# Reading the gates' destination scores from PSUM, and scatter sums that share one bank, in a graph layer

## The reference

```python
h = jnp.maximum(_layernorm(x, axis=-1), 0.0)
xs, xd = h[src], h[dst]
att = jax.nn.sigmoid(xs @ W_att[:d] + xd @ W_att[d:] + b_att)
messages = (xs @ W_msg + b_msg) * att
aggregated = jax.ops.segment_sum(messages, dst, num_segments=num_nodes)
gi = aggregated @ W_ih.T + b_ih
gh = h @ W_hh.T + b_hh
# r, z, n as in a GRU cell; h_new = (1 - z) * n + z * h
return x + gamma * (h_new - mean) * rsqrt(var + eps) + beta
```

## Time and profile before

| | us |
|---|---|
| median of 3 runs | 2257.26 |
| lowest and highest | 2253.13, 2259.02 |
| span of the profiled execution | 2256.1 |
| TensorE's granted clock in it, mean | 0.965 of full |

### The profile page before, as it was taken

One profiled execution on the slowest core, in us unless ns is written; L12 is line 12 of the kernel. 1 busy time (PEld: TensorE's weight loads), 2 busy tenths in 40 slices (PEclk: granted clock), 3 DMA queues, 4 the chain that ended last, 5 costly groups with the idle time before them and its releaser, 6 DMA issues.

```text
span 2256.1 us, 53903 instructions
## 1 busy us (share of the span) xinstructions
PE 2055.7 (91%) x18202; PEld 1994.3 (88%) x18202; DVE 2012.9 (89%) x4413; ACT 1996.3 (88%) x6980; POOL 1660.4 (74%) x1578
## 2 busy tenths in 40 slices
PE   3536999999999999999999999999999999999997
PEld 3525999999999999999999999999999999999996
DVE  5967899999999999999999999999999999999974
ACT  1368999999999999999999999999999999999943
POOL 4575777777777777777777777777777777777760
PEclk8865999999999999999999999999999999999998
DMA  6862222222222222222222222222222222222236
GB/s 164 237 172 62 56 60 62 59 60 60 62 62 62 63 58 64 61 63 59 63 59 62 59 61 60 63 60 62 60 61 63 59 62 60 61 61 64 58 108 231
DMA packets 167473, 171.57 MB, mean 76 GB/s; under 512 B 79462, under 2 KB 131736, under 8 KB 166944
## 3 DMA queue, kind: packets, MB, share of 16 engines
q0 software_dynamic: 49856, 102.96, 20.3%
q1 hardware_dynamic: 114564, 61.63, 10.5%
q10 hardware_dynamic: 2776, 3.52, 0.7%
HBM read 141.32 MB, written 26.65 MB: 74 GB/s over the span
## 4 chain that ended last, share of the span: by engine, by line
ACT 53%; PE 23%; DVE 14%; issue 7%; DMA 2%; SPq 1%; POOL 0%; ACTq 0%; DVEq 0%
ACT big L901 41%; PE ps L1456 12%; ACT gate_ring L897 9%; DVE big L1200 4%; PE ps L1441 4%; PE ps L1451 3%; DVE gate_ring L1184 2%; DVE key_hot L1170 1%; PE ps L1462 1%; PE ps L1463 1%; DVE lo_hot L1163 1%; DMA big<-in_x_dram 1%; DVE big L1129 1%; DMA row_ring<-node_table,set_idx 1%; ACT n_blk L906 1%
## 5 line engine op out<-in xcount | busy, mean ns | idle before, releaser
L773 POOL DMA_INDIRECT row_ring<-node_table,set_idx x1480 | 1571.8, 1062 | 473.4 <-issue 334.5
L901 ACT ACTIVATE big<-set_score,big 128x128 f32<-128x128 f32 x5096 | 1633.2, 394 | 81.0 <-PE ps L1456 80.7
L1456 PE MATMUL ps<-big 128*128 128x128 f32 x10192 | 1447.4, 281 | 0.0
L1456 PEld LDWEIGHTS ps<-big 128*128 128x128 f32 x10192 | 1265.0, 193 | 0.0
L1200 DVE TENSOR_TENSOR big<-ps,big 128x784 f32<-128x784 f32 x832 | 802.0, 964 | 10.2 <-ACT big L901 5.4
L1441 PE MATMUL ps<-gate_ring,row_ring 128*128 128x64 f32 x2960 | 534.8, 263 | 78.0 <-DVE gate_ring L1184 72.7
L1441 PEld LDWEIGHTS ps<-gate_ring,row_ring 128*128 128x128 f32 x2960 | 454.0, 194 | 124.4 <-DVE gate_ring L1184 110.7
L1184 DVE SCALAR_TENSOR_TENSOR gate_ring<-lane,set_rel,gate_ring 128x64 f32<-128x64 f32 x1480 | 412.9, 279 | 140.1 <-ACT gate_ring L897 135.0
L897 ACT ACTIVATE gate_ring<-set_win,row_ring 128x64 f32<-128x64 f32 x1480 | 493.2, 341 | 30.5 <-DMA row_ring<-node_table,set_idx 27.3
L1451 PE MATMUL ps<-key_hot,lo_hot 128*128 128x196 bf16 x3328 | 425.8, 250 | 14.4 <-DVE key_hot L1170 9.5
L1170 DVE TENSOR_TENSOR key_hot<-lane_key,set_key 128x1568 bf16<-128x1568 bf16 x416 | 402.0, 966 | 0.0
(11 more groups left out here) (129 smaller groups left out, 917.2 us busy)
## 6 DMA issues: line engine op xcount, KB each, us to landing
row_ring<-node_table,set_idx POOLq DMA_INDIRECT x1480
big<-in_x_dram SPq DMA_DIRECT2D x48, 256.0 KB, 5.6
h_blk<-hT_spill SPq DMA_DIRECT2D x97, 64.0 KB
node_table<-big SPq DMA_DIRECT2D x24, 258.0 KB
hT_spill<-big SPq DMA_DIRECT2D x24, 256.0 KB, 4.8
out_dram<-big SPq DMA_DIRECT2D x24, 256.0 KB
set_win<-dst_scores SPq DMA_DIRECT2D x148, 32.0 KB
set_score<-dst_scores SPq DMA_DIRECT2D x52, 64.0 KB
```

The source lines that it names most:

```text
L773: nc.gpsimd.indirect_dma_start(row_ring[:, t % ROWS_RING, :], None, table, bass.IndirectOffsetOnAxis(ap=set_idx[:, t // SET % 2, t % SET:t ...
L901: return nc.scalar.activation(a_buf[b % 2][:, h, :], set_score[:, b % 2, :], ACT.Sigmoid, bias=m_all[:, h, D:ROW])
L1456: return nc.tensor.matmul(ps[:, AM_BANK, 0:P], m_all[:, h, 0:D], a_buf[b % 2][:, h, :], start=h == 0, stop=h == HI - 1)
```

## The change

ACT copies what the gates read into PSUM. `keep_score(b)` copies the 128 destination scores of block `b` into bank 6 (two places, `ps_score`), once a block; `keep_window(g)` copies the 64 scores of group `g`'s window into the same bank (four places, `ps_dst_scores`), once a group, in the step of the group before's fifth tile. `gate` and `dense_gate` read these in place of `set_win` and `set_score`. SP's next `load_score` waits for the copy, not for the block's gates.

Bank 6 is thereby taken from the scatter sums. All groups now sum in bank 5, in four places of 64 columns (`ps_window`). `GROUP_LAG` goes from 3 to 1: DVE adds a group in the step of the next group's first tile, right after that tile's mask, when the group's last tile may just have been scattered. PE doesn't scatter the next group's first tile in its own step but one tile later, ahead of the second tile (`scattered_at`), and waits there until the group before has been added; before, it waited for the group before that one.

```diff
-GROUP_LAG = 3
+GROUP_LAG = 1
+def scattered_at(t):
+    if t < GROUP or t % GROUP > 1:
+        return (t,)
+    return (t - 1, t) if t % GROUP else ()
...
+        def ps_window(g):
+            return ps[:, SP_BANK, (g % GROUPS_S) * WIN:(g % GROUPS_S + 1) * WIN]
+        def ps_score(b):
+            return ps[:, SCORE_BANK, (b % 2) * P:(b % 2 + 1) * P]
+        def ps_dst_scores(g):
+            return ps[:, SCORE_BANK, 2 * P + (g % GROUPS_S) * WIN:2 * P + (g % GROUPS_S + 1) * WIN]
...
-                    sp.wait_ge(gates_dense, u + 1)
+                    sp.wait_ge(scores_kept, u + 1)
                     load_score(u + 2)
...
+            def keep_score(b):
+                act.wait_ge(score_loaded[b % 2], 16 * (b // 2 + 1))
+                nc.scalar.copy(ps_score(b), set_score[:, b % 2, :]).then_inc(scores_kept, 1)
+            def keep_window(g):
+                if g % GROUPS_S == 0:
+                    set_ready(act, g // GROUPS_S)
+                nc.scalar.copy(ps_dst_scores(g), set_win[:, g // GROUPS_S % 2, g % GROUPS_S, :]).then_inc(windows_kept, 1)
             def gate(t):
-                if t % SET == 0:
-                    set_ready(act, t // SET)
+                if t % GROUP == 0:
+                    act.wait_ge(windows_kept, t // GROUP + 1)
...
-                nc.scalar.activation(gate_ring[:, t % GATES_RING, :], set_win[:, t // SET % 2, t % SET // GROUP, :], ACT.Sigmoid,
+                nc.scalar.activation(gate_ring[:, t % GATES_RING, :], ps_dst_scores(t // GROUP), ACT.Sigmoid,
+                if t % GROUP == 4 and t // GROUP + 1 < GROUPS:
+                    keep_window(t // GROUP + 1)
             def dense_gate(b, h):
-                return nc.scalar.activation(a_buf[b % 2][:, h, :], set_score[:, b % 2, :], ACT.Sigmoid, bias=m_all[:, h, D:ROW])
+                return nc.scalar.activation(a_buf[b % 2][:, h, :], ps_score(b), ACT.Sigmoid, bias=m_all[:, h, D:ROW])
...
             def add_group(g, base):
-                nc.vector.tensor_tensor(window, ps[:, SP_BANK + g % 2, 0:WIN], window, ALU.add).then_inc(groups_added, 1)
+                nc.vector.tensor_tensor(window, ps_window(g), window, ALU.add).then_inc(groups_added, 1)
...
-                        if t % GROUP == GROUP_LAG and t > GROUP:
+                        if t % GROUP == 0 and t:
                             add_group(t // GROUP - 1, bases[t // GROUP - 1])
...
                 if t % GROUP == 0:
-                    wait_reuse(pe, groups_added, g - 1)
+                    wait_reuse(pe, groups_added, g)
...
-                        scatter(t)
+                    for of in scattered_at(t) if t is not None else ():
+                        scatter(of)
```

More of the change, by code:

```diff
@@ L70, in groups_before @@
 def groups_before(u, s):
-    return GROUPS if u == BLOCKS and s > LAST_TILES + GROUP_LAG else max(0, tiles_before(u, s) - GROUP_LAG - 1) // GROUP
+    return GROUPS if u == BLOCKS and s > LAST_TILES + GROUP_LAG else max(0, tiles_before(u, s) - GROUP_LAG) // GROUP
+def scattered_at(t):
+    if t < GROUP or t % GROUP > 1:
+        return (t,)
+    return (t - 1, t) if t % GROUP else ()
 def groups_needed(j):
@@ L315, in gnn_program @@
         ps = ctx.enter_context(nc.psum_tensor("ps", [P, 8, 512], F32))
-        AM_BANK, SP_BANK, GRU_BANK = 4, 5, 7
+        AM_BANK, SP_BANK, SCORE_BANK, GRU_BANK = 4, 5, 6, 7
         def ps_rows(b, j):
@@ L386, in gnn_program @@
         score_loaded = sems("score_loaded", 2)
+        scores_kept = sem("scores_kept")
+        windows_kept = sem("windows_kept")
         gathered = sems("gathered", ROWS_RING)
@@ L913, in _ @@
             keep_edges(11)
-            act.wait_ge(score_loaded[0], 16)
+            keep_score(0)
+            act.wait_ge(scores_kept, 1)
             act.wait_ge(sparse_stored, 32)
             for h in range(HI):
+                if h == HI - 6 * GATES_EARLY:
+                    keep_window(0)
                 if h == HI // 2:
@@ L937, in _ @@
                     b, i = dense_at(u, s)
+                    if u == 0 and s == 4:
+                        keep_score(1)
+                    if 0 < b < BLOCKS - 1 and i == 20:
+                        keep_score(b + 1)
                     if 0 < b < BLOCKS and i < PARTS:
                         if i == 0:
-                            act.wait_ge(score_loaded[b % 2], 16 * (b // 2 + 1))
+                            act.wait_ge(scores_kept, b + 1)
                         if b > 1:
@@ L1187, in add_group @@
             def add_group(g, base):
[L1189 removed]
+                dve.wait_ge(tiles_summed, (g + 1) * GROUP)
                 wait_reuse(dve, groups_added, g)
                 window = agg[:, bass.ds(base, WIN)]
[L1192 removed]
+                nc.vector.tensor_tensor(window, ps_window(g), window, ALU.add).then_inc(groups_added, 1)
             def keep_pairs(b, q):
@@ L1439, in scatter @@
                 if t % GROUP == 0:
-                    wait_reuse(pe, groups_added, g - 1)
-                nc.tensor.matmul(ps[:, SP_BANK + g % 2, 0:WIN], row_ring[:, t % ROWS_RING, 0:D],
+                    wait_reuse(pe, groups_added, g)
+                nc.tensor.matmul(ps_window(g), row_ring[:, t % ROWS_RING, 0:D],
                                  gate_ring[:, t % GATES_RING, :], start=t % GROUP == 0, stop=t % GROUP == GROUP - 1
@@ L1482, in _ @@
                     t = tile_at(u, s)
-                    if t is not None:
-                        scatter(t)
+                    for of in scattered_at(t) if t is not None else ():
+                        scatter(of)
                     if u < BLOCKS and s % PER_BEAT in (0, 2):
```

1 line of the change is left out of this document (removed).

## The result

| | us |
|---|---|
| before, median of 4 runs | 2257.89 |
| after, median of 4 runs (lowest, highest) | 2275.70 (2270.50, 2281.81) |
| ratio, 95% interval | 1.0087 [1.0072, 1.0103] |
| span of the profiled execution after | 2268.8 |

What follows compares the result with a forecast made beforehand. POOL's gathers, 38.6 us a block, and ACT's loop with PE at about that pace were taken as bounds. From a span of 2256.1 us, -12 at the start and -8 in pace gave 2236, so 2237 us; range 2198 to 2268.

Steps and rivals of the forecast that it cites:

- What bounds the kernel before: Block loop: POOL gathers without a stop, 38.6 us a block, and ACT's loop with PE closes at about that pace.
- the loss: What a batch's gathers lose beside DVE's one-hots: 0.43 us before, forecast to fall by 0.02 us a batch.
- ACT's reads: Gates reading PSUM save 0.042 us each, 5.3 us a block; the added copies cost 1.0 us a block.
- ACT's busy time: Sign expected in the profile: ACT some 12 points less busy, with dense gates 0.25 us apart.
- Start, -12 us: Up to 360 us: faster gates cut POOL's waits for scatters, 12 us saved, bounds -4 and -22.
- The end: After the last gather: the late landing of the last rows keeps its length, 0 us.
- Pace, -8 us: Block loop: one batch in ten more has a wait between lo and key one-hots, 0.35 becoming 0.16 us; 8 us saved.
- POOL gets slower: Rival, block loop: waits between one-hots vanish, gathers lose 0.50 us a batch, 2274 us; chance 0.15.
- The moved adding, 0 on the path: Group ends: 51 of 146 make DVE wait, 32 us in all, taken up by DVE's slack; 0 on the path.
- the slot that is freed later: Group's first tile: its row's slot is freed about 1 us later in one tile of ten; 0 us.
- PE takes over: Rival, block loop: gathers lose 0.33 us a batch, PE sets the pace, 2207 us, 2188 at bare pace; chance 0.20.

Runs made afterwards that it cites:

- e13: The kernel before with every second gather left out, all other work kept: 2257.64 us, 0.9980 of the kernel before.
- e5: The changed kernel run again without any edit: 2277.75 us, 1.0068 of the kernel before.
- e8: The kernel before with lo one-hots moved into step 3, right ahead of the key one-hots, in every batch: 2295.42 us, 1.0144 of the kernel before.
- e15: The changed kernel with the adding one tile later and the next group's first three scatters together behind it: 2278.80 us, 1.0081 of the kernel before.
- e14: The changed kernel with every second gather left out, all other work kept: 2232.52 us, 0.9881 of the kernel before.
- e6: The changed kernel with gates read from SBUF again and no copies, shared bank and new order kept: 2271.72 us, 1.0041 of the kernel before.
- e16: The kernel before with lo one-hots one step earlier: 2294.89 us, 1.0147 of the kernel before.
- e18: The kernel before with lo one-hots ahead of step 2's mask only where step 3 has no tile: 2296.30 us, 1.0170 of the kernel before.
- e1: A run on the slow chip where the kernel before takes 2572.41 us; the text does not say outright which edit it has.
- e9: The kernel before with every second gather left out, on the chip where the kernel before takes 2610.44 us: 2318.40 us, 0.8883.
- e3: The kernel before with lo one-hots one step earlier, on the slow chip where the kernel before takes 2572.41 us: 2593.05 us, 1.0071.
- e12: The kernel before with lo one-hots one step earlier, on the slow chip where the kernel before takes 2610.44 us: 2630.00 us, 1.0073.
- e4: The kernel before with lo one-hots right ahead of the key one-hots, where the kernel before takes 2572.41 us: 2582.53 us, 1.0031.
- e17: The changed kernel with lo one-hots ahead of step 2's mask only where step 3 has no tile: 2273.31 us, 1.0062 of the kernel before.

## Why the prediction was wrong

**What bounds the kernel before.** Right. It said that POOL never waits and sets 38.6 us a block, that ACT's loop with PE closes at about the same pace, and that both bound the kernel. e13 shows them within 4 us of each other over the whole kernel. That POOL takes no wait between two gathers is true in before, after, e5, e8 and e15, and where it is, the time must follow the loss. Against before, e8's loss of +0.085 us is +35 us by 416 batches, and +35 was measured; after's +0.060 is +25, less 4 from the start, and +18 was measured.

**ACT's reads.** Right. In the changed kernel, where one sparse gate and six dense ones repeat (start us, us):

```profile
159.18 0.40 ACT L926 ACTIVATE gate_ring<-ps,row_ring 128x64 f32<-128x64 f32 x1
159.38 1.75 ACT L932 ACTIVATE big<-ps,big 128x128 f32<-128x128 f32 x6
160.88 0.46 ACT L926 ACTIVATE gate_ring<-ps,row_ring 128x64 f32<-128x64 f32 x1
```

A dense gate every 1.50 / 6 = 0.25 us where it was 0.292, a sparse gate 0.20 where it was 0.24. Over the whole loop the median distance of starts fell from 0.292 to 0.250 us behind dense gates and from 0.239 to 0.197 behind sparse ones, so the unseen 64-wide form also saves 0.04. The copies take 0.14 and 0.20 us by the same measure (64 and 128 columns), 0.6 us a block where 1.0 was assumed. ACT's busy time fell by 6 points and not the 12 that I named, since the recorded duration of a gate grew to 0.44 us in the loop (0.39 before) while the starts moved closer: busy time of overlapping instructions is no measure of pace. The Trainium skill (VectorE: DVE Perf Modes, the section on the TRN2 errata) gives 52 cycles less for a PSUM source at 1.2 GHz, 0.043 us as an estimate; both shapes agree. That part of the gain is real and shows in e14.

**Start, -12 us.** Mis-sized. POOL's waits for scatters before 360 us fell from 36.8 to 25.2 us (net of 0.305 each, 22.5 to 13.0). By gather 200 the changed kernel is 4.2 us ahead (442.2 against 446.4 us), the prediction's lower bound for this term; e5's trace has it level (447.0). The end, put at 0, was 3 us shorter in the profiled pair.

**Pace, -8 us.** This step failed. I expected a faster ACT to be held up by rows, and DVE therefore to wait for a gate between lo and key one-hots more often, which shields the gathers. Rows did hold ACT up, 148 times, but the batches with a wait between the one-hots fell from 100 to 52, and the loss rose from 0.43 to 0.49: +25 us instead of -8. ACT's late gates were many and short (281 waits of DVE, mean 0.4 us); now there are half as many, and longer ones (141, 71.2 us). That waits for rows come in bunches, as in the episode of the last section, may be why; no run isolates it. Nor was a wait worth what I took it for: the 0.16 us of such batches held in the kernel before and was 0.41 in the changed one. The prediction priced a batch by what its kind had lost before, and that price did not carry over; why it didn't stays open. The outcome stood in the prediction as the rival "POOL gets slower" with 0.50 us, 2274 us, deciding at 0.46, and a chance of 0.15. Measured were 0.49 and 2275.7. That 2274 is so close is partly luck: it takes 12 us off at the start, of which 4 at most came, and puts the loss 4 us too high. What I lacked for the choice was a reason for the sign of the change in these waits; I had none, and still wrote a gain.

**The moved adding, 0 on the path.** Also wrong, by 11 us (e6). DVE's waits at the adding are 24 us in e6 and 55 after, where the count gave 32. (In that count the last row shown should read 0.98 us and not 0.58: 2176.06 + 0.40 less 2175.28 + 0.20. A recount gives 52 ends and 34 us, so nothing hangs on it.) The slack of 2.3 us a block did take up DVE's own wait (e15), but not what a group's end does to `keep_pairs` and the build behind it (3.4 us of waits became 13.1), to the slot that is freed later (0 in the prediction, some 4 us of POOL's waits in e6) and to the gathers (loss 0.45 in e6). How the 11 us divide among these was not tested. e15 shows that the time doesn't come back when the adding gets more time.

**PE takes over.** Without POOL's limit PE with DVE stands at 2232 us (e14), not at 2207. Its waits for DVE (38.0 us for masks, 11 for `keep_pairs` in the loop) don't go away with POOL's limit, and the bare 37.4 us a block is not reached.

**The whole.** Without POOL's limit the change is worth 25 us (e14 against e13), and POOL, level with ACT's loop before, has become some 20 us slower by the same change. That the gathers are what holds the changed kernel is shown; that they got slower beside DVE's one-hots is shown by their lengths there and by e8; which part of the new order of waits made them slower is not.

## What to carry to other kernels

Where an engine never waits, leave out half of its work in an experiment before you call it the limit: another loop may stand within 0.2% of it, and the engine may also be slowed by what the faster one does. A wait that an edit removes may have left another engine undisturbed, so ask what ran freely beside it; but don't price the new waits by what the old ones did, since here 0.16 us a batch became 0.41. An edit that mends such a collision by reordering (e16 to e18) has a price at every engine that waits, directly or through another, for the instruction moved back: in the kernel before PE and through it ACT, 33 and 37 us.

## What the runs showed of the hardware that I had not expected

**TensorE's clock fell after several short waits.** One episode of the changed kernel. ACT, then DVE, then PE (start us, us, in brackets the idle time before):

```profile
946.48 0.31 ACT L926 ACTIVATE gate_ring<-ps,row_ring 128x64 f32<-128x64 f32 x1 [1.38 <-DMA row_ring<-node_table,set_idx]
...
948.96 0.31 ACT L926 ACTIVATE gate_ring<-ps,row_ring 128x64 f32<-128x64 f32 x1 [1.39 <-DMA row_ring<-node_table,set_idx]
...
949.31 0.28 DVE L1222 SCALAR_TENSOR_TENSOR gate_ring<-lane,set_rel,gate_ring 128x64 f32<-128x64 f32 x1 [1.31 <-ACT gate_ring L926]
...
949.65 0.43 PE L1480 MATMUL ps<-gate_ring,row_ring 128*128 128x64 f32 x2 [0.70 <-DVE gate_ring L1222]
950.62 0.50 PE L1490 MATMUL ps<-key_hot,lo_hot 128*128 128x196 bf16 x4 [0.54 <-DVE big L1239]
```

PE was busy 0.35, 0.46 and 0.32 us in the three us from 949, with no idle piece over 0.7 us. Then (stretch; length, PE busy, PEld, DVE, ACT, POOL, granted clock, DMA share, GB/s):

```profile
950.00:951.00 1.00, 0.46 (x5) 0.30 (x4) 0.95 (x3) 1.00 (x5) 0.70 (x2) 1.00 0.53 123
951.00:952.00 1.00, 0.32 (x3) 0.19 (x2) 0.70 (x4) 1.00 (x5) 0.69 (x2) 0.79 0.09 27
952.00:953.00 1.00, 0.50 (x2) 0.31 (x2) 1.00 (x3) 1.00 (x6) 0.70 (x2) 0.50 0.30 66
...
957.00:958.00 1.00, 1.00 (x7) 1.00 (x6) 1.00 (x3) 0.01 (x1) 0.88 (x1) 0.50 0.33 70
958.00:959.00 1.00, 1.00 (x9) 1.00 (x10) 0.79 (x3) 0.82 (x3) 0.69 (x2) 0.80 0.53 116
959.00:960.00 1.00, 1.00 (x12) 1.00 (x12) 0.14 (x1) 0.88 (x4) 0.69 (x2) 1.00 0.05 12
```

The granted clock is half, 1.2 GHz, until 958 us, PE making 7 matmuls a us where it makes 12 at 2.4 GHz. Of the 179 stretches of 10 us, 5 are below 0.97 in the kernel before and 9 in the changed one (13 in e5), 9 against 15 us of clock. With PE's idle time, 59 against 69 us, that is some 16 us more in PE's books, where 22 were counted at POOL: two sides of one loss, not to be added. That waits for rows come in bunches was seen in this episode; I didn't count bunches.

**Chips differ by 14 to 16%.** The same kernel takes 2258 to 2262 us in the first runs and those of e5 to e8 and e13 to e18, on at least two chips, and 2572 and 2610 on two others. On the slow ones the whole loop is slower with all gathers, and was not with half (seen on one of the two). Stretch from 360 to 2150 us in e1 (on one of them), columns as above:

```profile
360.00:2150.00 1790.00, 1615.34 (x13738) 1545.02 (x13737) 1478.07 (x3058) 1523.34 (x5342) 1194.64 (x1146) 0.96 0.25 53
```

and in e9, half the gathers, on the other:

```profile
360.00:2150.00 1790.00, 1731.54 (x15781) 1691.45 (x15780) 1669.98 (x3513) 1721.42 (x6135) 726.62 (x658) 1.00 0.17 37
```

15,781 matmuls in 1,790 us is the pace of the good chips (15,739 in the kernel before); 13,738 is not. On these chips lo one-hots a step earlier cost the kernel before 0.7% (e3, e12), not 1.5% (e16), and lo late 0.3% (e4), not 1.4% (e8): POOL waits there anyway, 246 us in e4's stretch from 360 to 2150 us. Why the chips differ stays open.

**What else stays open.** Why DVE's waits between the one-hots fell rather than rose, and why batches with one lose more than before, is not shown; no run sets these waits by hand. Half the gathers on top of e6 and of e17, which would price the moved adding and the edit of e17 by themselves, were not run. Why POOL and ACT's loop stood level to 0.2% before was not tested. And the gates from PSUM with the adding left where it was, which might keep the 25 us without the 11, were not tried: the PSUM room for the copies is what the moved adding frees.
